# Column energies of criss-cross attention: the matmul reads its keys in place, 96 elements apart, in place of a Pool copy

## What is computed

```
q = einsum('oc,bchw->bohw', Wq, x) + bq          # 64 channels
k = einsum('oc,bchw->bohw', Wk, x) + bk          # 64 channels
v = einsum('oc,bchw->bohw', Wv, x) + bv          # 512 channels
energy_H = einsum('bchw,bcgw->bhwg', q, k) - 1e30 * eye(H)[None, :, None, :]
energy_W = einsum('bchw,bchv->bhwv', q, k)
att = softmax(concatenate([energy_H, energy_W], -1), -1)
att_H, att_W = att[..., :H], att[..., H:]
out_H = einsum('bcgw,bhwg->bchw', v, att_H)
out_W = einsum('bchv,bhwv->bchw', v, att_W)
out = gamma * (out_H + out_W) + x
```

## Time and profile before

| | before |
|---|---|
| median of 3 runs | 3756.95 us (3755.92 to 3760.14) |
| profiled execution, its own time | 3755.24 us |
| span of the trace | 3753.5 us, granted TensorE clock 0.996 |
| PE busy | 98% of the span, 26992 matmul instructions |
| DVE, ACT, POOL busy | 72%, 41%, 17% |
| DMA engines, mean share | 76% |

### The profile page before, as it was taken

How to read it: one execution, slowest core, us unless ns; L and a number is a source line. 1 busy time by engine, 2 the same in 40 slices (tenths; PEclk the granted TensorE clock), 3 DMA queues, 4 the chain that set the end, 5 groups by cost and what they waited for, 6 DMA issues and landing times.

```text
span 3753.5 us, 67076 instructions
## 1 busy us (share of the span) xinstructions
PE 3680.6 (98%) x26992; PEld 3663.1 (98%) x26992; DVE 2686.3 (72%) x4324; ACT 1526.3 (41%) x2130; POOL 644.8 (17%) x793
## 2 busy tenths in 40 slices
PE   7799999999999999999999999999999999999999
PEld 7799999999999999999999999999999999999999
DVE  8766777677876778767786677866778667786555
ACT  8523444234542445424454244542444424444111
POOL 0410023100331003210032100421004200042000
PEclk9899999999999999999999999999999999999999
DMA  8687768877688776977759777697775977769665
GB/s 266 163 238 255 245 213 228 237 254 258 201 235 242 252 245 202 248 242 243 259 183 260 237 252 244 195 251 241 243 259 183 253 239 259 230 198 260 213 211 175
DMA packets 330500, 873.97 MB, mean 233 GB/s; under 512 B 34256, under 2 KB 182224, under 8 KB 330192
## 3 DMA queue, kind: packets, MB, share of 16 engines
q1 hardware_dynamic: 330192, 869.67, 75.8%
HBM read 661.92 MB, written 207.62 MB: 232 GB/s over the span
## 4 chain that ended last, share of the span: by engine, by line
PE 93%; DVE 4%; DMA 1%; issue 1%; ACT 0%; POOL 0%; DVEq 0%; SPq 0%; ACTq 0%; POOLq 0%
PE bank L955 42%; PE bank L922 18%; PE bank L943 17%; PE bank L873 10%; PE bank L883 3%; PE bank L892 3%; DMA XT_r<-in_x_row 1%; DVE E L657 1%; DVE Sx L636 1%; DVE Sx_first L636 0%; DVE zs_c L667 0%; DVE Sy L641 0%; DVE mx_c L652 0%; DVE mx_r L652 0%; DVE zs_r L667 0%
## 5 line engine op out<-in xcount | busy, mean ns | idle before, releaser
L955 PE MATMUL bank<-Sy,Wv_hi 128*128 128x384 f32 x6144 | 1593.6, 340 | 12.9 <-DVE Sy L641 11.9
L955 PEld LDWEIGHTS bank<-Sy,Wv_hi 128*128 128x128 f32 x6144 | 1087.2, 188 | 15.2 <-issue 13.1
L955 PE MATMUL bank<-Sy,Wv_lo 128*128 128x384 f32 x3072 | 1027.6, 335 | 0.0
L729 DVE SCALAR_TENSOR_TENSOR Y<-bank,bv_sb,Y 128x384 f32<-128x384 f32 x768 | 469.6, 612 | 702.2 <-PE bank L955 702.2
L422 POOL TENSOR_TENSOR Pe<-Pe,F 96x384 f32<-96x384 f32 x384 | 323.2, 843 | 2514.2 <-DMA Pe<-e_scratch 2473.6
L943 PE MATMUL bank<-Pt,XT_r 128*128 128x96 f32 x6144 | 717.4, 274 | 2.7 <-DMA XT_r<-in_x_row 2.4
L943 PEld LDWEIGHTS bank<-Pt,XT_r 128*128 128x128 f32 x6144 | 713.7, 192 | 4.1 <-DMA XT_r<-in_x_row 4.0
L539 ACT ACTIVATE Sy<-Y 128x768 fp32r<-128x768 f32 x384 | 302.9, 835 | 888.0 <-PE bank L955 861.4
L955 PEld LDWEIGHTS bank<-Sy,Wv_lo 128*128 128x128 f32 x3072 | 576.6, 188 | 0.0
L530 ACT ACTIVATE Y<-bank 128x384 f32<-128x384 f32 x384 | 325.4, 847 | 436.7 <-PE bank L922 436.7
L713 DVE COPY Y<-bank 128x384 f32<-128x384 f32 x384 | 318.0, 828 | 217.0 <-PE bank L922 198.4
(11 more groups left out here) (66 smaller groups left out, 2838.7 us busy)
## 6 DMA issues: line engine op xcount, KB each, us to landing
XT_r<-in_x_row SPq DMA_DIRECT2D x384, 384.0 KB, 6.0
Y<-in_x SPq DMA_DIRECT2D x192, 768.0 KB, 5.8
out<-Y SPq DMA_DIRECT2D x192, 768.0 KB, 4.2
XA<-in_x SPq DMA_DIRECT2D x180, 768.0 KB, 6.8
XT_r<-in_x_col SPq DMA_DIRECT2D x192, 384.0 KB, 7.8
XT_c<-in_x_col SPq DMA_DIRECT2D x192, 384.0 KB, 7.6
e_scratch<-E SPq DMA_DIRECT2D x384, 144.0 KB, 3.1
Pe<-e_scratch SPq DMA_DIRECT2D x384, 144.0 KB, 7.5
```

Source lines behind the costliest of these rows:

```text
L729: nc.vector.scalar_tensor_tensor(at, proj_ps[c % 2][:, 0:CP], bv_sb[:, c:c + 1], at, op0=ALU.add, op1=ALU.add).then_inc(out_made, 1)
L955: last = nc.tensor.matmul(proj_ps[c % 2][:, 0:CP], w[:, ct, at], Sy[:, lo, ct, :], start=(ct == 0 and k == 0), stop=(ct == CT - 1 and k == 2))
```

## The change

Column energies no longer use a gathered copy of the keys. `column_energies` takes the moving operand from KQ through a view in which the index along a column is last, so that the 96 elements of one matmul lie 96 elements apart, and all 128 partitions are read (the queries in partitions 64 to 127 meet the zeros of Q, as in `row_energies`). The four matmuls of a group are otherwise the same. `gather_k` and `zero_kg` are gone from POOL, with the semaphores k_gathered and kg_zeroed. PE now waits for kq_evicted once, at the image's first group. The scratch use of Kg moves to a tile of its own, Fs, of 2 x 288 elements in the same slot.

```diff
--- before.py
+++ after.py
@@ -83,7 +83,7 @@
             Sx = sb("Sx", [P, 2, CT, CP], F32R, s1)
             E = sb("E", [P, ERING, CP], F32, s1)
             KQ = sb("KQ", [P, POS], F32, s1)
-            Kg = sb("Kg", [P, 2, CP], F32, s1)
+            Fs = sb("Fs", [P, 2, BLOCKS * N], F32, s1)
             st = sb("st", [P, 4, N], F32, s1)
             mx_c = sb("mx_c", [P, N], F32, s1)
             zs_c = sb("zs_c", [P, N], F32, s1)
@@ -94,7 +94,7 @@
             raw_v = sb("raw_v", [P, CT, C], F32, s2)
             raw_qk = sb("raw_qk", [P, CT, P], F32, s2)
         Y = sb("Y", [P, CHUNKS + 1, CT, CP])
-        SX_SLOTS, E_SLOT, KQ_SLOT, KG_SLOT = (2, 3), 4, 5, 11
+        SX_SLOTS, E_SLOT, KQ_SLOT, FS_SLOT = (2, 3), 4, 5, 11
 
         Wv_hi = sb("Wv_hi", [P, CT, C], F32R)
         Wv_lo = sb("Wv_lo", [P, CT, C], F32R)
@@ -163,12 +163,12 @@
         wqk_in, wv_in, small_in = sem("wqk_in"), sem("wv_in"), sem("small_in")
         w_hi_made, w_lo_made, gbv_made = sem("w_hi_made"), sem("w_lo_made"), sem("gbv_made")
         ident_made, zeros_made = sem("ident_made"), sem("zeros_made")
-        xt_zeroed, kg_zeroed = sem("xt_zeroed"), sem("kg_zeroed")
+        xt_zeroed = sem("xt_zeroed")
         xa_in = [sem(f"xa_in{j}") for j in range(2)]
         xa_first_in = [sem(f"xa_first_in{j}") for j in range(4)]
         x_hi_made, x_lo_made, x_half_used = sem("x_hi_made"), sem("x_lo_made"), sem("x_half_used")
         qk_summed, kq_evicted = sem("qk_summed"), sem("kq_evicted")
-        q_gathered, k_gathered = sem("q_gathered"), sem("k_gathered")
+        q_gathered = sem("q_gathered")
         e_summed, e_maxed, e_shifted = sem("e_summed"), sem("e_maxed"), sem("e_shifted")
         e_exped, c_masked, z_summed = sem("e_exped"), sem("c_masked"), sem("z_summed")
         e_stored = [sem(f"e_stored{j}") for j in range(ERING)]
@@ -190,7 +190,7 @@
         by_pe = (x_half_used, qk_summed, e_summed, o_summed, proj_summed)
         by_act = (x_hi_made, kq_evicted, q_gathered, e_exped, c_moved_act, y_hi_made)
         by_dve = (x_lo_made, e_maxed, e_shifted, z_summed, p_turned, c_moved_dve, r_added, y_lo_made, out_made, f_made)
-        by_pool = (k_gathered, c_masked, p_scaled)
+        by_pool = (c_masked, p_scaled)
         START = {**{s: 16 for s in by_dma}, **{s: 8 for s in (*by_pe, *by_act, *by_dve, *by_pool)}}
 
         def past(s, n):
@@ -389,22 +389,6 @@
             for s in by_pool:
                 pool.sem_inc(s, START[s])
 
-            def gather_k(a, g):
-                if g == 0:
-                    pool.wait_ge(kq_evicted, past(kq_evicted, (a + 1) * CHUNKS))
-                    pool.wait_ge(kg_zeroed, a + 1)
-                pool.wait_ge(e_summed, past(e_summed, e_no(a, CHUNKS + g - 2)))
-                src = KQ[0:CQ, :].rearrange("p (h w) -> p w h", w=N)[:, g * ROWS:(g + 1) * ROWS, :]
-                nc.gpsimd.tensor_copy(Kg[0:CQ, g % 2, :].rearrange("p (w h) -> p w h", w=ROWS), src)\
-                    .then_inc(k_gathered, 1)
-
-            def zero_kg(a, before=True):
-                if before:
-                    out_landed(pool, a - 1, KG_SLOT)
-                    pool.wait_ge(p_scaled, past(p_scaled, p_no(a - 1, CHUNKS + B_FIRST + 3)))
-                nc.gpsimd.memset(Kg[CQ:P, :, :], 0.0).then_inc(kg_zeroed, 1)
-                pool.wait_ge(kg_zeroed, a + 1)
-
             def mask(a, g):
                 pool.wait_ge(e_exped, past(e_exped, e_no(a, CHUNKS + g)))
                 at = by_block(E[0:N, g % ERING, :])
@@ -436,19 +420,11 @@
                 scale(b, CHUNKS + 3)
                 for n in range(CHUNKS):
                     b_now = b_groups(n) if more else []
-                    if b_now and b_now[0] == 0:
-                        zero_kg(b + 1)
-                        gather_k(b + 1, 0)
-                        gather_k(b + 1, 1)
                     for g in b_now[:3]:
-                        if g + 2 < CHUNKS:
-                            gather_k(b + 1, g + 2)
                         mask(b + 1, g)
                     if n + 4 < CHUNKS:
                         scale(b, CHUNKS + n + 4)
                     for g in b_now[3:]:
-                        if g + 2 < CHUNKS:
-                            gather_k(b + 1, g + 2)
                         mask(b + 1, g)
 
             def prologue():
@@ -462,12 +438,7 @@
                 nc.gpsimd.memset(Pt[N:P, :, :], 0.0).then_inc(zeros_made, 1)
                 nc.gpsimd.memset(XT_r[N:P, :, :, :], 0.0).then_inc(zeros_made, 1)
                 pool.wait_ge(zeros_made, 3)
-                zero_kg(0, before=False)
-                gather_k(0, 0)
-                gather_k(0, 1)
                 for g in range(CHUNKS):
-                    if g + 2 < CHUNKS:
-                        gather_k(0, g + 2)
                     mask(0, g)
 
             def whole(b):
@@ -540,7 +511,7 @@
 
             def choose_factors(a):
                 act.wait_ge(e_summed, past(e_summed, e_no(a, 2 * CHUNKS - 1)))
-                nc.scalar.activation(Kg[0:N, 0, 0:BLOCKS * N].rearrange("k (q b p) -> k q b p", q=BLOCKS, b=BLOCKS),
+                nc.scalar.activation(Fs[0:N, 0, :].rearrange("k (q b p) -> k q b p", q=BLOCKS, b=BLOCKS),
                                      per_block(ident[:, :]), ACT.Copy).then_inc(f_chooser, 1)
 
             def factors(a):
@@ -648,7 +619,7 @@
                 m = mx(along)[:, n * ROWS:(n + 1) * ROWS]
                 dve.wait_ge(e_summed, past(e_summed, e_no(a, i)))
                 if i == CHUNKS and before:
-                    out_landed(dve, a - 1, KG_SLOT)
+                    out_landed(dve, a - 1, FS_SLOT)
                 nc.vector.tensor_reduce(m, ps, AX_X, ALU.max).then_inc(e_maxed, 1)
                 if i == 0 and before:
                     out_landed(dve, a - 1, E_SLOT)
@@ -692,7 +663,7 @@
                 dve.wait_ge(st_step, steps + 7)
                 nc.vector.tensor_tensor(st[0:N, 1, :], st[0:N, 1, :], st[0:N, 3, :], ALU.mult).then_inc(f_ready, 1)
                 nc.vector.tensor_tensor(
-                    Kg[0:N, 1, 0:BLOCKS * N].rearrange("k (q b p) -> k q b p", q=BLOCKS, b=BLOCKS),
+                    Fs[0:N, 1, :].rearrange("k (q b p) -> k q b p", q=BLOCKS, b=BLOCKS),
                     per_block(st[0:N, 2, :]), per_block(st[0:N, 3, :]), ALU.mult).then_inc(f_ready, 1)
 
             def take_factors(a, along):
@@ -886,11 +857,13 @@
 
             def column_energies(a, g):
                 pe.wait_ge(q_gathered, past(q_gathered, a * CHUNKS + g + 1))
-                pe.wait_ge(k_gathered, past(k_gathered, a * CHUNKS + g + 1))
+                if g == 0:
+                    pe.wait_ge(kq_evicted, past(kq_evicted, (a + 1) * CHUNKS))
                 pe.wait_ge(e_shifted, past(e_shifted, e_no(a, CHUNKS + g - 2)))
+                columns = KQ[:, :].rearrange("p (h w) -> p w h", w=N)
                 for r in range(ROWS):
                     last = nc.tensor.matmul(ec_ps[g % 2][0:N, r * N:(r + 1) * N], Q[:, g % 2, r * N:(r + 1) * N],
-                                            Kg[:, g % 2, r * N:(r + 1) * N], start=True, stop=True)
+                                            columns[:, g * ROWS + r, :], start=True, stop=True)
                 last.then_inc(e_summed, 1)
 
             def turn_stats(a):
@@ -904,7 +877,7 @@
                 if not along:
                     pe.wait_ge(f_chooser, a + 1)
                 for q in range(BLOCKS):
-                    last = nc.tensor.matmul(f_ps[along][:, q * N:(q + 1) * N], Kg[0:N, along, q * N:(q + 1) * N],
+                    last = nc.tensor.matmul(f_ps[along][:, q * N:(q + 1) * N], Fs[0:N, along, q * N:(q + 1) * N],
                                             ident[:, :] if along else st[0:N, 1, :], start=True, stop=True)
                 last.then_inc(f_turned, 1)
 
```

## The result

| | before | after |
|---|---|---|
| median | 3756.57 us (3755.92 to 3760.14, 4 runs) | 3856.38 us (3855.60 to 3856.69, 4 runs) |
| span of the trace | 3753.5 us | 3854.4 us |
| granted TensorE clock | 0.996 | 0.996 |

The change makes the kernel slower: ratio 1.0265, 95% interval 1.0253 to 1.0277, or 100.9 us more by the two spans. The forecast was 3877 us, the likeliest case's own range 3838 to 3895, and the whole range 3748 to 3895.

A forecast was written before the change was run, and what follows sets the result against it. PE was taken to bound the kernel, busy 98% of the span. The profiled 3755.24 us plus 120.2 for the strided read, 0 for everything else, and 1.7 to the median gave 3877 us; range 3748 to 3895.

The forecast's parts named there:

- likeliest case: Row-stage column energies: a strided element costs PE 1.5 to 1.8 ns; 3838 to 3895 us, chance 0.48.
- POOL's copies, the waits, the zeros, Fs: Removed POOL work, altered PE waits, zeros met by queries, Fs replacing Kg as scratch: each predicted to change the time by 0.
- The moving operand: Row-stage column energies: each of 1344 matmuls grows from 84.6 to 174 ns through the strided read, +120 us.
- Whoever asks: Assumption that SBUF hands any engine one 16-byte piece in about 1.8 ns, so a strided element costs PE 1.81 ns.
- read twice: Column-energy matmuls: PE fetches strided elements twice per instruction, 348 ns; +354 us in row stages, 4140 us total, chance 0.10.
- Free: Row-stage column energies: strided element served within 0.88 ns, hidden by the small matmul; 3745 to 3760 us, chance 0.30.
- The prologue: Prologue's 192 column-energy matmuls: groups grow 0.7 us, hidden by 1.2 us of cover; cost 0, or 17 us if uncovered.
- Partly hidden: Row-stage column energies: another engine's stride surcharge atop PE's 0.45 ns, 110 to 139 ns a matmul; 3791 to 3830 us, chance 0.12.

The follow-up runs named there:

- e1: The changed kernel without POOL's copies, but PE reads 96 keys side by side in KQ (not the column's keys): 3754.59 us, ratio 0.9996 to the kernel before.
- e3: The changed kernel with moving-operand steps of 96, 1, 2, 3, 4, 6, 16, 96 elements for images 0 to 7: 3825.54 us, single run.
- e4: The kernel before; last image's row stage only: row attention with moving, weight or both steps 4, projection with moving steps 2, 3, 4, 96: 3855.79 us, single run.
- e6: The kernel before; last image's row stage only: row attention with moving or weight step 2, projection with moving steps from 2 to 192: 3802.09 us, single run.
- e2: The kernel before, POOL's copies and PE's wait kept, only the column energies' moving operand read from KQ at step 96: 3858.18 us, ratio 1.0273.
- e5: The changed kernel, but ACT copies keys instead of queries and PE loads queries from KQ as weights, 96 apart: 3850.95 us, ratio 1.0252.

## Why the prediction was right, and where it was off

**POOL's copies, the waits, the zeros, Fs: 0.** Right as a sum. e1 has all of them and takes the time of the kernel before. That DVE sets the period in the prologue was right too. But the prediction named ACT's copy as what would be late next for PE, and it is DVE's subtraction. The earlier trace rows had it already: L657 ends at 107.83 and ACT's copy at 107.71. PE therefore came 0.35 us earlier, not 0.6, which changed nothing in the sum. In the row stages it was said that ACT's copy is early; PE has no wait for it.

**The moving operand: +120 us.** The mechanism, a read in place on PE that costs by the piece, was right, and the size too large: the term measures 0.62 us for a group, 104 us, and the whole change 100.9. What was off is the price of an element, taken as 1.81 ns from ACT's read and PE's 16 bytes. At step 96 a matmul takes 165 ns by the chain and not 174, 1.72 ns an element; that is 12 us of the gap of 19. The work behind it gains back 0.03 us a group, some 4 us. The 1.81 was near for steps 3, 4 and 6 (1.81, 1.78 and 1.79 in e3); why 16 and 96 are some 4% cheaper is open. Another 4.5 us are PE's waits that the slower matmuls covered, which the sum did not have. With the 0.5 us of the prologue these make 21 us, within 2 us of the gap.

**"Whoever asks".** The reasoning behind the 1.8 ns was only partly right. e4 shows a strided element served to PE in 0.90 ns in the one-pass projection. The numbers of e3, e4 and e6 up to step 48 are described within 7% by one rule, fitted to them afterwards: a visit to a 16-byte piece costs 0.9 ns for a single access and 1.8 ns for two to four, and a float32 matmul accesses each element twice in a row. In order that is 4 accesses a piece in the projection (96 x 1.81 = 174). At step 4 it is one access there (384 x 0.90 = 347) and two in float32 (96 x 1.78 = 171). At step 2 it is four in float32 (48 pieces, 86 ns, hidden). That each element is accessed twice was not seen directly; it is what makes the numbers agree. If it holds, the rival "read twice" had a grain of truth, at half the price that I gave an access. "Free" argued that the second access costs nothing, and e3 shows the surcharge from step 3 on. That ACT's 1.82 ns an element came near the true number was partly luck: PE serves an element in 0.90 ns in one kind of matmul and in 1.78 in the other, and nothing here shows that ACT pays for the same reason.

The Trainium skill's page "SBUF — State Buffer", section "Specifications (TRN2)", asks for two hits in a 16-byte line. The float32 matmul agrees (step 2: 86 against 85 ns), the one-pass projection does not: at step 2 it has two hits in each line and takes 341 ns, not 174. The rule of the page "TensorE: Matmul & The Clock Gate", section "Step-by-step: what each phase is for", that streaming takes a cycle a column, does not give the time of a strided read: the same 96 columns took 85 to 172 ns in e3, by the step alone.

**The prologue: 0.** Right: the groups kept their 1.58 us and 0.5 us came back. The cover was smaller than the 1.2 us of the prediction: 0.35 us of earlier start (e1) and 0.57 us at DVE make 0.92, a group grew by 0.6, and PE's loads still wait 0.36 us between groups.

**The other cases.** "Free" would have needed 0.88 ns an element; e2 and e3 show 1.72. "Partly hidden", a surcharge on top of 0.45 ns, gave at most 139 ns; it was 165. "Read twice" at 348 ns did not come.

No version here beats the kernel before. e1 shows why sparing POOL's copies cannot: they cost the kernel nothing that can be told, and both ways of sparing them (the changed kernel and e5) put 94 to 100 us on PE.

## What to carry to other kernels

A copy that only puts data side by side, made by an engine that nobody waits for, is cheap; reading with a step on the engine that bounds the kernel is paid in full, here twice the time of each float32 matmul. Price a strided operand of a float32 matmul by the 16-byte pieces that it touches: step 2 was free and everything from step 4 cost about the same. The one-pass projection was already at half pace at step 2. Before taking work off an engine, look whether the engine that waits for it would not wait for the next one at the same moment.

## What was not expected of the hardware

- A one-pass matmul over 384 elements took 174 ns in order and 325 to 353 ns at steps 2 to 48, but 205 ns where only four pieces alternate and 168 where two do, less than in order.
- Strided weights cost as much as a strided stream: 233 ns for 128 weights at step 4, 117 at step 2; both strided together also 233. In e5 weights with a step of 96 came 165 ns apart, like the stream with a step of 96.
- Groups of 32 matmuls with strided weights brought the granted clock from 1.00 to 0.50 for a few us, 0.87 on average in the projections between them, though PE never idled; groups of 8 (e5) did not.
